# Blocks' loads, gathers and routing steps in another order, and expert weights in two transfers

## Time and profile before

| | |
|---|---|
| three runs | 1988.4, 1993.6, 1996.0 us |
| profiled execution | 1995.9 us |
| its span, first to last instruction | 1994.2 us |
| mean granted TensorE clock | 0.876 |
| PE busy | 1511.0 us (76%) |
| PEld busy | 1256.6 us (63%) |
| DVE busy | 975.6 us (49%) |
| ACT busy | 759.6 us (38%) |
| POOL busy | 442.1 us (22%) |
| moved by DMA | 331.7 MB, mean 166 GB/s |

### The profile page before, as it was taken

One profiled execution on the slowest core, in us unless ns is written; L12 is line 12 of the kernel. 1 busy time (PEld: TensorE's weight loads), 2 busy tenths in 40 slices (PEclk: granted clock), 3 DMA queues, 4 the chain that ended last, 5 costly groups with the idle time before them and its releaser, 6 DMA issues.

```text
span 1994.2 us, 30357 instructions
## 1 busy us (share of the span) xinstructions
PE 1511.0 (76%) x9344; PEld 1256.6 (63%) x9344; DVE 975.6 (49%) x3299; ACT 759.6 (38%) x2327; POOL 442.1 (22%) x422
## 2 busy tenths in 40 slices
PE   7999999999973418788457977827898787877760
PEld 6998898898873317667336766615666565655540
DVE  5777777777773302411336562425855333243315
ACT  5565565555530104345243543304344232223320
POOL 1010100000006470000515134261511503122015
PEclk9999999999986658799779988868998897888885
DMA  8265256246002142699637575421755664177743
GB/s 314 113 244 188 71 225 241 69 173 242 1 1 92 59 146 60 201 301 309 210 119 252 165 219 187 141 82 60 244 164 183 219 196 144 59 251 229 229 154 94
DMA packets 173078, 331.71 MB, mean 166 GB/s; under 512 B 17280, under 2 KB 85888, under 8 KB 171680
## 3 DMA queue, kind: packets, MB, share of 16 engines
q1 hardware_dynamic: 157600, 288.31, 43.4%
q0 software_dynamic: 15360, 41.96, 6.5%
HBM read 196.41 MB, written 133.27 MB: 165 GB/s over the span
## 4 chain that ended last, share of the span: by engine, by line
PE 45%; DVE 15%; issue 10%; DMA 8%; another core or an unknown queue 8%; ACT 7%; POOL 4%; SPq 2%; DVEq 0%; ACTq 0%; POOLq 0%
PE psum L407 37%; DMA xb<-xs 8%; PE psum L1579 2%; POOL xs L618 2%; POOL og L633 2%; PE psum L1401 1%; ACT p_sb L730 1%; DVE x L1095 1%; PE psum L1550 1%; SPq L505 1%; DVE s_sb L1123 1%; PE psum L1412 1%; DVE stats L940 1%; ACT p_sb L728 1%
## 5 line engine op out<-in xcount | busy, mean ns | idle before, releaser
L407 PE MATMUL psum<-xbT,bw 128*96 128x128 f32 (+1 forms) x2392 | 338.6, 293 | 0.0
L407 PEld LDWEIGHTS psum<-xbT,bw 128*96 128x96 f32 (+1 forms) x2392 | 312.8, 194 | 0.6 <-issue 0.3
L633 POOL DMA_INDIRECT og<-l_os,l_back_of x160 | 161.4, 1009 | 575.0 <-DMA l_os<-b_out 310.1
L407 PE MATMUL psum<-bw,b_act 96*128 96x256 f32 (+2 forms) x692 | 229.1, 424 | 63.9 <-ACT b_out L803 20.0
L1111 DVE TENSOR_TENSOR b_act<-psum,b_gated 96x128 f32<-96x128 f32 x190 | 53.9, 286 | 370.4 <-ACT b_gated L790 338.5
L618 POOL DMA_INDIRECT xs<-x,row_of x160 | 159.9, 1000 | 236.3 <-DVE row_of L1026 189.4
L1106 DVE TENSOR_TENSOR b_act<-psum,b_gated 128x128 f32<-128x128 f32 x126 | 36.7, 291 | 343.0 <-ACT b_gated L787 298.4
L779 ACT ACTIVATE xbT<-psum 128x256 f32<-128x256 f32 x252 | 96.3, 382 | 249.1 <-PE psum L1579 230.1
L407 PEld LDWEIGHTS psum<-bw,b_act 96*128 96x128 f32 (+2 forms) x692 | 113.6, 206 | 103.5 <-issue 75.9
L407 PE MATMUL psum<-l_shared_w,b_act 128*128 128x256 f32 (+1 forms) x192 | 70.9, 467 | 128.4 <-DVE b_act L1111 50.1
L1579 PE MATMUL psum<-ident,xb 128*128 128x128 f32 x504 | 110.2, 302 | 75.6 <-DMA xb<-xs 71.1
(11 more groups left out here) (217 smaller groups left out, 3706.8 us busy)
## 6 DMA issues: line engine op xcount, KB each, us to landing
xs<-zeros SPq DMA_DIRECT2D x42, 1792.0 KB, 17.3
bw<-l_w SPq DMA_DIRECT2D x94, 640.0 KB
bw<-l_w SPq DMA_DIRECT2D x158, 320.0 KB
xb<-xs SPq DMA_DIRECT2D x252, 128.0 KB
l_os<-b_out SPq DMA_DIRECT2D x124, 256.0 KB
decay_all<-decay_dram SPq DMA_DIRECT2D x32, 384.0 KB
aw_raw<-attn_w SPq DMA_DIRECT2D x8, 1024.0 KB, 6.9
xs<-x,row_of POOLq DMA_INDIRECT x160
```

What stands on the lines that cost most here:

```text
L407: last = nc.tensor.matmul(out_ap, w, m, start=start and n == 0, stop=stop and n == len(pairs) - 1, **kw)
L633: pool.indirect_dma_start(og[:, i % MIX_RING, k, :], None, os[f["layer"]][t // HALF_TILES], bass.IndirectOffsetOnAxis(ap=back_of[f["layer" ...
```

## The change

In words, and in the order of the diff:

- The list: layer 1's shared blocks of half 1 move from ahead of its routed blocks to the end (now 300 to 315; the routed ones of half 1 are 253 to 299).
- The slots: 102 in a span, pairs begin at 18 and 50, and the second span ends eight blocks before layer 1's second half of routed blocks (at 245).
- Layer 0's gathers go out two DMAs a slot, over three slots a tile (`GATHERED`); a combine is done in two halves at two slots (`COMBINED`).
- Layer 1's combines of half 0 are every fifth block from 261 on; four of half 1 are at blocks 305, 308, 310 and 312, within the shared blocks, the last four after the last block. Gathers are queued three blocks ahead of their combine.
- The loads: `block_load` is split into `weights_load` and `rows_load`. Rows are issued six blocks ahead (fewer at the start of a half), weights six in layer 0 and three in layer 1; of one iteration rows come first. For the first half of a layer the first seven (or four) weights are issued at once, five blocks ahead.
- A block's weights are two transfers. Layer 0: gate and up of all partitions (128 x 384 floats), down of the 96 partitions that hold something (96 x 256). Layer 1: everything but the second part of down (128 x 1024), and that part for partitions 64 to 127 (64 x 256). Before, it was one transfer of 128 x 640 and 128 x 1280. PE waits for 32 instead of 16 on the same semaphore.
- Layer 1's scatter for the first pair of a half is issued one DMA a slot from o = 48 to 63; the second pair's stays whole.
- `weights` is split into `weights_sum`, `rows_back` and `weights_of`, done at three successive blocks; layer 1's four quads are now at 1, 4, 10 and 15 blocks behind block 253.
- `choose` of layer 1 moves from o = 44 to 45, `rank` from 45 to 46, and `slots`, `count`, `table`, `rows_turn`, `rows_read` by one or two behind it.

The core of the diff:

```diff
-    if _f is L1:
-        FIRST["shared", _h] = len(STREAM)
-        STREAM += shared_blocks(L1, range(HALF_TILES * _h, HALF_TILES * (_h + 1)))
+    if (_f, _h) == (L1, 0):
+        FIRST["shared", 0] = len(STREAM)
+        STREAM += shared_blocks(L1, range(HALF_TILES))
     FIRST[_f["layer"], _h] = len(STREAM)
     STREAM += routed_blocks(_f, _h)
+FIRST["shared", 1] = len(STREAM)
+STREAM += shared_blocks(L1, range(HALF_TILES, TILES))
...
-FRONT = 8, 40
-SLOTS = 90
-SPAN = (FIRST[0, 1], FIRST["shared", 0]), (FIRST["shared", 0], FIRST["shared", 1])
+FRONT = 18, 50
+SLOTS = 102
+SPAN = (FIRST[0, 1], FIRST["shared", 0]), (FIRST["shared", 0], FIRST[1, 1] - 8)
...
+GATHERED = 0, 3, 6, 9, 18, 21, 27, 31
+COMBINED = (4, 5), (7, 8), (10, 11), (13, 14), (25, 26), (28, 29), (32, 34), (37, 38)
...
-    return TAIL + 2 + 4 * j
+    return TAIL + 8 + 5 * j if j < HALF_TILES else FIRST["shared", 1] + (5, 8, 10, 12)[j - HALF_TILES]
+
+
+def load_at(n):
+
+    f, h, m, _ = STREAM[n]
+    first = FIRST[f["layer"], h]
+    if f is L0:
+        weights = first - 5 if h == 0 and m < L0_RING - 1 else n - 6
+    else:
+        weights = first - 5 if h == 0 and m < L1_RING else n - 3
+    return weights, max(n - 6, first - 4 + m // 2)
+
+
+LOADS = {}
+for _n in ROUTED:
+    for _kind, _at in zip(("weights", "rows"), load_at(_n)):
+        LOADS.setdefault(_at, []).append((_kind, _n))
+
+
+def weigh_at(f, q):
+
+    return FIRST[0, 0] + 4 + 4 * q if f is L0 else TAIL + (1, 4, 10, 15)[q]
...
-                sp.dma_start(bw[:, k * f["cols"]:(k + 1) * f["cols"]],
-                             expert_w[f["layer"]][bass.ds(row >> REGION_BITS, 1)].rearrange("a p w -> p (a w)")).then_inc(bw_loaded[k], 16)
+                whole, kept = (slice(0, f["down"] + D), slice(HALF, P)) if f["layer"] else (slice(0, f["down"]), slice(0, f["width"]))
+                of_block = expert_w[f["layer"]][bass.ds(row >> REGION_BITS, 1)].rearrange("a p w -> p (a w)")
+                to = bw[:, k * f["cols"]:(k + 1) * f["cols"]]
+                sp.dma_start(to[:, whole], of_block[:, whole]).then_inc(bw_loaded[k], 16)
+                sp.dma_start(to[kept, whole.stop:], of_block[kept, whole.stop:]).then_inc(bw_loaded[k], 16)
...
-            for n in range(-4, BLOCKS + 1):
-                for lead, f in ((4, L0), (3, L1)):
-                    if 0 <= n + lead < BLOCKS and is_routed(n + lead) and STREAM[n + lead][0] is f:
-                        block_load(n + lead)
+            for n in range(BLOCKS + 1):
+                for kind, b in LOADS.get(n, ()):
+                    if kind == "rows":
+                        rows_load(b)
+                for kind, b in LOADS.get(n, ()):
+                    if kind == "weights":
+                        weights_load(b)
...
+                rows = [(t, k) for t in range(QUAD * q, QUAD * (q + 1)) for k in range(f["top"])]
+                for t, k in rows if part is None else rows[part:part + 1]:
+                    pool.indirect_dma_start(xs[q // 2], bass.IndirectOffsetOnAxis(ap=row_of[:, t, k:k + 1], axis=0), x[:, t, :], None) \
+                        .then_inc(scattered[q], 16)
...
+            def gather(f, t, ks):
 
                 i = f["layer"] * TILES + t
-                wait(pool, combined, i - MIX_RING + 1)
-                for k in range(f["top"]):
+                if ks[0] == 0:
+                    wait(pool, combined, i - MIX_RING + 1)
+                for k in ks:
...
+                        if 0 <= v - GATHERED[j] < 3:
+                            k = 2 * (v - GATHERED[j])
+                            gather(L0, HALF_TILES * h + j, (k, k + 1))
...
-                    if n == FIRST[0, 0] + 4 + 4 * q:
-                        weights(L0, q)
-                    if n == (FIRST["shared", 1] + 2 + 4 * q if q < 2 else TAIL + 4 * q):
-                        weights(L1, q)
+                for f in LAYERS:
+                    for q in range(QUADS):
+                        if n == weigh_at(f, q):
+                            weights_sum(f, q)
+                        if n == weigh_at(f, q) + 1:
+                            rows_back(f, q)
+                        if n == weigh_at(f, q) + 2:
+                            weights_of(f, q)
...
+                        for part in range(2):
+                            if v == COMBINED[j][part]:
+                                combine(L0, HALF_TILES * h + j, range(3 * part, 3 * part + 3))
...
-                    pe.wait_ge(bw_loaded[k], 16 * turn + 16)
+                    pe.wait_ge(bw_loaded[k], 32 * turn + 32)
```

More of the change, by code:

```diff
@@ L609, in _, with scatter @@
             low_part(GROUPS - 1, 3)
[L611 to L616, removed]
-                    for k in range(f["top"]):
-                        pool.indirect_dma_start(xs[q // 2], bass.IndirectOffsetOnAxis(ap=row_of[:, t, k:k + 1], axis=0), x[:, t, :], None) \
-                            .then_inc(scattered[q], 16)
+            def scatter(f, q, part=None):
+                if part in (None, 0):
+                    if f["layer"] == 0 and q == 0:
+                        pool.wait_ge(xs_zeroed, 16 * ZEROED * (GROUPS - 1))
+                    pool.wait_ge(placed, QUADS * f["layer"] + q + 1)
+                rows = [(t, k) for t in range(QUAD * q, QUAD * (q + 1)) for k in range(f["top"])]
+                for t, k in rows if part is None else rows[part:part + 1]:
+                    pool.indirect_dma_start(xs[q // 2], bass.IndirectOffsetOnAxis(ap=row_of[:, t, k:k + 1], axis=0), x[:, t, :], None) \
+                        .then_inc(scattered[q], 16)
             def all_stored(f, h):
@@ L1067, in weights, with rows_back @@
                 chained(dve.tensor_tensor(wn, wn, per_row(row_stat[:]).to_broadcast([P, QUAD, e]), ALU.mult))
+            def rows_back(f, q):
+                e, top, h = f["experts"], f["top"], q // 2
+                tiles = slice(QUAD * q, QUAD * (q + 1))
                 of = by_expert(place, f)[:, tiles, :]
@@ L1076, in weights, with weights_of @@
                 dve.tensor_scalar(back_of[f["layer"]][:, tiles, 0:top], places[:, tiles, 0:top], -1.0, None, ALU.add)
+            def weights_of(f, q):
+                e, top = f["experts"], f["top"]
+                tiles = slice(QUAD * q, QUAD * (q + 1))
+                wn = weight[:, :, 0:e]
+                hit = hits[:, 0:QUAD * top * e].rearrange("p (i k e) -> p i k e", k=top, e=e)
                 for i in range(QUAD):
@@ L1097, in combine @@
                         chained(ins)
[L1098 to L1099 removed]
+                if ks[-1] == f["top"] - 1:
+                    ins.then_inc(combined, 1)
+                    dve.wait_ge(combined, i + 1)
             def block_act(n):
@@ L1339, in _ @@
                             ln_rows(1, p)
-                for j in range(HALF_TILES):
+                for j in range(HALF_TILES + QUAD):
                     if n == tail_mix(j):
-                        combine(L1, j)
+                        combine(L1, j, range(L1["top"]))
                 for q in range(2):
@@ L1348, in _ @@
             for q in range(2, QUADS):
-                for t in range(QUAD * q, QUAD * (q + 1)):
-                    combine(L1, t)
+                if q == QUADS - 1:
+                    for t in range(QUAD * q, QUAD * (q + 1)):
+                        combine(L1, t, range(L1["top"]))
                 ln_stats(q, combined, TILES + QUAD * (q + 1))
```

74 lines of the change are left out of this document (36 added, 38 removed).

## The result

The changed kernel takes 1866.5 us (median of 1863.1 to 1876.5) beside 1994.8 for the kernel before on the same chip: ratio 0.9368, 95% interval 0.9321 to 0.9415. That is 128 us less, where 162 were forecast. The profiled execution took 1863.1 (span 1861.4, granted clock 0.905 against 0.876).

A forecast was written before the change was run, and what follows sets the result against it. From 786.2 us no engine was taken as full; PE was busiest, 868 of 1208 us, with about 340 us of stalls. Terms (a) to (i) summed to -162 us: 1834 profiled, 1832 as median, range 1765 to 1912.

The forecast's parts named there:

- (c): First turn of `x` at 957 us comes 13 us earlier, seven more blocks under the wait: gain 22, ends 5 and 35.
- (f): Turn at 1285 us, behind 16 scatters and 24 gathers, comes earlier with four more blocks under it: gain 26, ends 8 and 40.
- (h): Layer 1's shared blocks moved last, with nothing but gathers beside them: gain 7 us, ends 0 and 15.
- (a): `weights` in three pieces removes four PE stalls in layer 0: gain 12, ends 0 and 17; layer 1 cost 4.
- (b): Second weight transfer makes SP take 1.9 to 2.1 us a block in layer 0's first half: cost 4, 0 to 11.
- (d): Scatter of quarters 0 and 2, one DMA a slot, removes two PE waits for mask products: gain 26, ends 14 and 30.
- (e): `choose` one slot after the group scores and `rank` one later shorten PE's waits: gain 6 us, ends 0 and 12.
- (g): Last expert stage: rows issued six blocks ahead leave the chain, 3.4 us a block: gain 40, ends 18 and 60.
- (i): Tail: gathers and combines moved into the shared blocks, leaving 31 us against 62.5: gain 31, ends 26 and 34.
- POOL's streak costing the same: Rival: (c), (f), (h) at weak ends and (d) at 14, -108 us, 1888; chance 0.18.
- Weights in the place of rows: Rival: weights become what is late, (g) at 18 and (b) at 11, -133 us, 1863; chance 0.10.
- The slower case: Rival: second transfer lands 2.4 us behind the first in layer 1's 94 blocks, 226 us added, 2060; chance 0.06.

The follow-up runs named there:

- chip B: Kind of chip without late PE results; unedited kernels rerun there: changed 1712.8 us, ratio 0.9295; kernel before 1839.4 us in the profiled run.
- chip A: Kind of chip with late PE results, that of the result: kernel before 1994.8 us, changed kernel 1866.5 us, ratio 0.9368.
- spread_alone: Kernel before with only the scatters of quarters 0 and 2 issued one DMA a slot: 1969.5 us beside 1999.0, ratio 0.9836.
- loads_old: Changed kernel with a block's weights and rows issued together again, weights first, four or three blocks ahead: 1923.0 us beside 1999.0, ratio 0.9617.
- best: Changed kernel with layer 0's weights in one transfer and layer 1's quarter 1 scatter behind the first gathers: 1860.1 us beside 1999.0, ratio 0.9309.

## Why the prediction was right, and where not

**The whole.** 1832 was forecast, 1866 came, inside 1765 to 1912. The forecast's steps hold but for two, (c) and (f), with (h) too small. In part the nearness is luck: the two mixed stages gained 29 us where 80 were forecast, and some 20 us more than forecast came in the others.

**(a)** 12 forecast, 12 measured. (By the stretch it was read from the stalls cost 18 us, not 17: 52 us less 17.7 blocks of 1.91.) The 4 us for layer 1 didn't come: in one piece there it is no better (158.0 against 155.4).

**(b)** 4 forecast, 10.8 in its stage and 7 in the whole: the upper bound. SyncE as the limit was right, at 2.04 us a block of the 1.9 to 2.1 forecast. The price was too low because it was set against 1.91 us, while one transfer a block goes at 1.87; and bytes weren't what counted, for DMA-engine time a block didn't fall at all.

**(c) and (f)** are the steps that failed. The chain of 24 gathers, combine and norm was worked out nearly rightly: 47.5 us forecast, 49.8 without late results (its combine of six is 3.1 us at the rate named, not 3.5). What failed was "13 us" against the earlier trace rows: I compared a chain without lateness with a trace that had it. The kernel before has the same chain, 49.0. So the order of the gathers brought nothing to the first turn, on either chip. What gain there is, with (e), is 32 us on chip B and not 54, probably by the seven blocks under the wait, and only beside (d). In (f) 54 was forecast and 57.2 came on chip B, but 77.2 on chip A. On the chip of the result (d) alone had shortened the two stages by 25.2 us of the 29.0, so some 4 us are left for (c), (e) and (f), between two sets: less than their weak ends, 5, 0 and 8, together.

**(d)** 26 forecast; 33 (23 to 43) alone, 42 with the rest. Right in the mechanism and a little low. No wait for `mix` in the changed kernel is over 2.1 us.

**(e)** 6 forecast. The whole run's waits of the ranks, against the earlier trace rows:

```profile
PE psum L426 <- DVE prefix L1046: 9.2, 6, 1.9
```

6.8 us less, by these; on chip B the waits of this kind fell from 21.7 to 11.1 us. No run has (e) by itself.

**(g)** 3.4 us a block forecast, 3.40 measured (159.7 / 47); 36 us forecast with (a)'s part, 41.6 measured. PE is the bound there now.

**(h)** 7 forecast, 18.9 on chip A, 5.5 on chip B (46.9 to 41.4). In the old place a scatter of 16 ran beside these blocks, with PE's results up to 9.6 us late on chip A, which is likely the difference; no run took it apart.

**(i)** 31 forecast, 30.8 measured, and 29.9 on chip B. Neither (h) nor (i) was undone in a run; both are read from the stages.

**The rivals.** POOL's streak costing the same was right for (c) and (f), not for (h) and (d), and so the profiled 1863 lies between it (1888) and the forecast (1834). Weights in the place of rows (1863) came near the time by chance: (g) was full. The slower case, 2.4 us for each second transfer, did not come, since both land together. The Trainium skill, SBUF — State Buffer, "Who interferes with whom", has PE and ScalarE never waiting for others at SBUF's ports, which I took to put (c) and (f) at their strong ends. They didn't get there even on the chip where nothing is late; and on the other PE's results are late in POOL's streaks only, by whatever link.

## What to carry to other kernels

Before a wait is credited to an order of work, recompute the old chain by the same rates as the new: what the old trace has above it is something else, and may stay. Where the DMA engines are full, count packets by their time and not bytes, and ask whether the issuing queue keeps any slack. An in-order queue that carries both long streaks of DMAs and small products somebody waits for is worth spreading out; and where two such parts lie in one stage, undo each and compare with the sum, for each may be worth nothing without the other.

## What the runs showed of the hardware

On chip A PE's semaphore updates come late while POOL issues indirect DMAs in a long run. I count an update as late when it comes over 1 us behind the last recorded end of a PE instruction that gives it. In the five traces from chip A (before, changed, spread_alone, loads_old, best) 290 are late; all but two became due within a run of two or more indirect DMAs on POOL or 2 us behind it, and most in the long ones. In runs of 12 or more, 1.27 us apart, the worst was 41.4 us (the 48 DMAs of layer 0's scatter) and in most of them over 4; in runs of six to eleven at most 8.8; and when the 16 DMAs of a scatter go out by ones to fours (changed kernel, 1165 to 1205) 1.2. Of the updates of VectorE, ScalarE and POOL in the same traces one is late, by 1.2 us. In the eight traces of chip B with runs as long, at the same pace, there is none of PE's (the resets in a trace's last 2 us left out). This is a correlation over kernels that differ in much else; what the link is, and why one kind of chip has it, stays open. The chips differ by 147 us of 1995 for the kernel before and 154 of 1866 for the changed one. That all of this comes of the late updates isn't shown; it fits that the stages of the kernel before in which PE works and POOL has no long run take nearly the same on both (blocks 32 to 111, 169.0 and 169.8 us; the last routed blocks, 201.3 and 198.9).
